# Linear attention, cross attention and a top-1 expert layer: the spreading of the queries over the heads goes from Pool to VectorE

## The chip, the cores and the metric

The kernel runs on one core of one Trainium2 chip. The metric is the device time in microseconds; lower is better. A core has TensorE (PE, matrix products), VectorE (DVE), ScalarE (ACT), GpSimd (POOL), and queues of DMAs, here issued by SyncE (SP) and by Pool. Each engine takes its instructions in the order of its own program, and they meet only in semaphores.

## What is computed

x and the context hold 32 sequences of 128 tokens with 128 features. Three blocks follow each other, each with the residual and a layer norm behind it:

```python
# 1: causal linear attention, 16 heads of 8
q, k = relu(q) + 1e-6, relu(k) + 1e-6
kv    = cumsum(einsum('bhld,bhle->bhlde', k, v), axis=2)
k_cum = cumsum(k, axis=2)
out   = einsum('bhld,bhlde->bhle', q, kv) / maximum(einsum('bhld,bhld->bhl', q, k_cum)[..., None], 1e-6)
x = layernorm(x + out @ out_w.T + out_b)
# 2: cross attention to the context, softmax over keys at most 64 tokens away
x = layernorm(x + softmax(scores(x, ctx)) @ ctx_heads @ W_proj.T + b_proj)
# 3: 8 experts, each token to the best one, at most int(N / E * 1.25) + 1 tokens an expert
top1 = argmax(softmax(xf @ wg)); h = gelu(eb @ W1 + b1); y = h @ W2 + b2
x = layernorm(x + gathered * combine_w)
```

## The kernel before

The kernel is written by hand for each engine, with explicit semaphores. A first stage (up to about 380 us of the span) treats the sequences as a pipeline: round n handles sequence n in its first operations, sequence n - 1 in later ones, down to n - 8. `at(op, n - 2)` in an engine's loop emits the operation for sequence n - 2 if there is one. There are B + LAST = 40 rounds, and the order of the `at` lines is the order in which that engine works. The second stage is the expert layer.

In each round the following matters here (b is the sequence):

- TensorE makes q, k and v of sequence n (`op_qkv`, L567 to L569) into the bank "qkv".
- VectorE turns the bank into qT (L922), kT (L916) and, with the bias, the values V1 (`op_v`, L928).
- Pool spreads qT over the heads: QE (`op_QE`, L420) has 4 copies of qT[128, 128], each multiplied by a column of `head_mask`, so that a product with a group of 32 rows of kT sees one head of 8 rows alone. The two inputs are read with repetition: qT four times, and each of the 4 mask elements 128 times.
- TensorE's scores of the first attention (`op_s1`, L533 with QE and kT) use QE one round later, at n - 1.
- VectorE subtracts the mean and scales for the first layer norm: x1 of sequence n - 2 (`op_x1`, L1002), and for the second, x2 of sequence n - 7 (`op_x2`, L1032). Both are one operation from SBUF to SBUF of 128 x 128 in fp32, with two scalars per partition.
- TensorE transposes x1 (`op_x1T`, L526), then makes pv1 (L589), then the scores of the cross attention s2 (L533 with CE and x1T). VectorE copies the transposed x1 in between (`op_x1Te`, L1088). s2 claims the bank of the transpose too, and so waits for that copy.
- VectorE takes maxima over s2's banks (`op_mx0`, `op_mx1`, L1007) at the start of its next round.
- Pool in each round: x1 + bias (`op_x1b`, L431), the power -1/2 for x1 (L426), xb = X + bias (L409), the copy V2 of the context (L414), QE (L420), the power -1/2 for x2 and for the fallback (L437 to L446), and the scatter of x2 into the experts' rows (L453, a DMA).

VectorE's order around the change is ve1, q, k, lg5, n2, v, x1, x2, rk1, res2, x1Te. Pool's power for x1 waits for ve1 (L977), and xb, V2 and QE follow it. QE has two buffers and `op_q` of the next sequence waits for QE_ready.

Of the kernel before, what the change touches and what calls it, by code (L numbers as in the profile page):

```python
# [8 lines left out]
ALU = mybir.AluOpType  # L9
# [3 lines left out]
P = 128  # L13
# [13 lines left out]
class Seq:  # L27
# [10 lines left out]
    def wait(self, mark=None):  # L38
        self.eng.wait_ge(self.sem, self.n if mark is None else mark)
# [7 lines left out]
def decoder(nc, x, ctx_in, qkv_w, qkv_b, out_w, out_b, proj_w, proj_b, wg, W1, b1, W2, b2, out):  # L47
    B, T, D = x.shape
    E, _, F = W1.shape
    HD = 8  # L50
    H = D // HD
# [3 lines left out]
    NA = H // G  # L55
# [23 lines left out]
    with ctx:  # L79
        def sb(name, shape, dt=F32):  # L80
            return ctx.enter_context(nc.sbuf_tensor(name, shape, dt))

        def ring(name, n, shape, dt=F32):
            return [sb(f"{name}{k}", shape, dt) for k in range(n)]

        def sem(name):
            return ctx.enter_context(nc.semaphore(name))

        banks = ctx.enter_context(nc.psum_tensor("banks", [P, 8, 512], F32))
        BANKS = {name: used for name, _, used in JOBS}  # L90

        def bank(name):
            return banks[:, BANKS[name][0], :]

        def by_parity(V):

            return V[:].rearrange("p (s q) (u w) -> p s (q u) w", q=2, w=SLOT)[:, :, 0:4:3, 0:HD]
# [18 lines left out]
        head_mask = sb("head_mask", [P, NA])  # L116
# [23 lines left out]
        qT = ring("qT", 2, [P, P])  # L140
        kT = ring("kT", 2, [P, P])
        QE = ring("QE", 2, [P, NA, P])
# [102 lines left out]
        qkv_full, q_done, k_done, v_done = sem("qkv_full"), sem("q_done"), sem("k_done"), sem("v_done")  # L245
        QE_ready = sem("QE_ready")
        s1_full = sem("s1_full")
# [45 lines left out]
        def at(op, b):  # L293
            if 0 <= b < B:
                op(b)
# [75 lines left out]
        def _(pool):  # L371
            g = nc.gpsimd
# [41 lines left out]
                g.tensor_copy(by_parity(V2[b % 4]),  # L414
                              C[b % RX][:].rearrange("p (s q d) -> p s q d", q=2, d=HD)).then_inc(v2_ready, 1)

            def op_QE(b):
                pool.wait_ge(q_done, b + 1)
                wait(pool, s1_full, b - 1)
                g.tensor_tensor(QE[b % 2][:], qT[b % 2][:].unsqueeze(1).broadcast_to([P, NA, P]),  # L420
                                head_mask[:].unsqueeze(2).broadcast_to([P, NA, P]), ALU.mult).then_inc(QE_ready, 1)

            def op_pow1(b):
                pool.wait_ge(var1_ready, b + 1)
                wait(pool, x1_ready, b)
                g.tensor_tensor(rs1[:], ve1[:], minus_half[:, 0:1], ALU.pow).then_inc(rstd1_ready, 1)  # L426
# [30 lines left out]
            for n in range(B + LAST):  # L457
                at(op_x1b, n - 4)
                at(op_pow1, n - 2)
                at(op_xb, n)  # L460
                at(op_v2, n - 1)
                at(op_QE, n)
                at(op_pow2, n - 6)
                at(op_fbs, n - 6)
                at(op_scatter, n - 8)
# [416 lines left out]
        def _(dve):  # L882
            v = nc.vector
# [35 lines left out]
            def op_q(b):  # L919
# [2 lines left out]
                v.tensor_scalar(qT[b % 2][:], bank("qkv")[:, 0:P], qk_bias[:, 0:1], FEATURE_EPS, ALU.add,  # L922
                                ALU.max).then_inc(q_done, 1)

            def op_v(b):
                dve.wait_ge(qkv_full, b + 1)
                wait(dve, pv1_full, b - 1)
                v.tensor_tensor(by_parity(V1[b % 2]),  # L928
                                bank("qkv")[:, 2 * P:3 * P].rearrange("p (s q d) -> p s q d", q=2, d=HD),
                                v_bias[:].rearrange("p (s q d) -> p s q d", q=2, d=HD), ALU.add).then_inc(v_done, 1)  # L930
# [174 lines left out]
            for n in range(B + LAST):  # L1105
                at(op_mx0, n - 3)
                at(op_mx1, n - 3)
                at(op_den1, n - 2)
                at(op_rec1, n - 2)
                at(op_mxh, n - 3)  # L1110
                at(op_n1, n - 2)
                at(op_mxs, n - 3)
                at(op_y1Te, n - 2)
                at(op_lg1, n - 8)
                at(op_xTe, n)
                at(op_lg2, n - 8)
                at(op_lg3, n - 8)
                at(op_res1, n - 2)
                at(op_lg4, n - 8)
                at(op_st1, n - 2)  # L1120
                at(op_rec2, n - 4)
                at(op_mv1, n - 2)
                at(op_ve1, n - 2)
                at(op_q, n)
                at(op_k, n)
                at(op_lg5, n - 8)
                at(op_n2, n - 4)
                at(op_v, n)
                at(op_x1, n - 2)
                at(op_x2, n - 7)  # L1130
                at(op_rk1, n - 8)
                at(op_res2, n - 6)
                at(op_x1Te, n - 2)
                at(op_rk2, n - 8)
                at(op_st2, n - 6)
                at(op_rk3, n - 8)
                at(op_mv2, n - 6)
                at(op_rk4, n - 8)
                at(op_ve2, n - 6)
# [115 lines left out]
```

## Time and profile before

| | |
|---|---|
| median of 3 runs | 499.87 us (498.59 to 501.1) |
| the profiled execution: time, span of the core | 499.5 us, 497.6 us |
| busy in the span: TensorE, VectorE, ScalarE, Pool | 425.5, 358.0, 283.5, 247.6 us |
| mean granted clock of TensorE | 0.949 |
| steady rounds 100 to 300 us: TensorE, VectorE, ScalarE, Pool busy | 190.8, 171.4, 133.3, 102.9 of 200 us |
| QE on Pool | 32 times, mean 1032 ns |
| x1 and x2 on VectorE | 32 times each, mean 414 and 883 ns |

A busy engine need not be the bound: the ends of TensorE's products are modelled and overlap. The span leaves out a little at either end of the execution. In a timeline, an operation often starts up to 0.1 us before the one ahead of it on its engine has ended.

### The profile page before, as it was taken

The page shows a single profiled execution, that of the slowest core. Times are in us where ns is not written, and L with a number is a line of the kernel's source. Part 1 is how long each engine was busy: PE and PEld are TensorE (multiplying, and loading weights), DVE is VectorE, ACT ScalarE, POOL GpSimd, SP SyncE. Part 2 cuts the span into 40 slices and gives each one's busy share as a digit, 9 for nine tenths or more (in the row PEclk, how much of TensorE's full clock was granted, in tenths as well). Part 3 has the DMA queues.
Part 4 walks back from the last instruction along what each step waited for, and adds up shares of the span by engine and source line. Part 5 has one row for each costly group of instructions (what it writes and reads, how often), then busy time and mean ns, then how long its engine had stood idle before and what let it go on. Part 6 is the DMA issues. An engine that isn't in the chain of part 4 may idle for free. (4 is left out here: it accounts for less than half of the span.)

```text
span 497.6 us, 20822 instructions
## 1 busy us (share of the span) xinstructions
PE 425.5 (86%) x7767; PEld 335.0 (67%) x7767; DVE 358.0 (72%) x1680; ACT 283.5 (57%) x691; POOL 247.6 (50%) x420
## 2 busy tenths in 40 slices
PE   3879999999999999999999999998851699999930
PEld 2667777777777777777777777775641488888730
DVE  5255677788888788888788888887574267767740
ACT  1445667666766666767666766666242356666620
POOL 4132244554454554454554454553364036887883
PEclk9999999999999999999999999999775699999985
DMA  5700000101000101000101000000004333344100
GB/s 149 237 14 14 24 14 14 29 25 38 27 24 26 29 25 40 25 26 24 30 24 40 26 13 15 19 15 19 13 29 121 84 81 89 101 112 124 24 19 18
DMA packets 30901, 22.69 MB, mean 46 GB/s; under 512 B 4460, under 2 KB 27281, under 8 KB 30804
## 3 DMA queue, kind: packets, MB, share of 16 engines
q1 hardware_dynamic: 27604, 17.16, 12.3%
q0 software_dynamic: 3200, 4.22, 2.9%
q8 instruction: 63, 1.03, 0.9%
q14 instruction: 34, 0.28, 0.2%
HBM read 12.25 MB, written 9.65 MB: 44 GB/s over the span
## 5 line engine op out<-in xcount | busy, mean ns | idle before, releaser
L1007 DVE TENSOR_REDUCE mx<-banks 128x8 f32<-128x1024 f32 x64 | 75.4, 1219 | 37.8 <-PE banks L541 37.8
L797 ACT ACTIVATE arena<-banks 128x1024 f32<-128x1024 f32 x64 | 62.0, 1021 | 35.4 <-PE banks L541 35.4
L426 POOL TENSOR_TENSOR rs<-ve,minus_half 128x1 f32<-128x1 f32 x32 | 18.0, 564 | 115.5 <-DVE ve L977 115.5
L589 PE MATMUL banks<-arena,V 128*32 128x128 f32 x2048 | 70.0, 278 | 0.6 <-ACT arena L797 0.6
L767 ACT ACTIVATE arena<-banks,first_half 128x512 f32<-128x512 f32 x64 | 44.7, 698 | 32.8 <-PE banks L541 32.8
L589 PEld LDWEIGHTS banks<-arena,V 128*32 128x32 f32 x2048 | 52.6, 110 | 11.1 <-issue 8.9
L483 POOL DMA_INDIRECT out_x<-ot,idx x48 | 50.0, 1041 | 12.0 <-issue 10.2
L533 PE MATMUL banks<-CE,x1T 32*128 32x128 f32 x1024 | 37.5, 282 | 10.7 <-DVE x1T L1088 9.7
L437 POOL TENSOR_TENSOR rs<-ve,minus_half 128x1 f32<-128x1 f32 x32 | 17.9, 559 | 56.1 <-DVE ve L996 56.0
L745 PE MATMUL banks<-w_sb,arena 128*112 128x128 f32 (+1 forms) x384 | 44.0, 274 | 0.9 <-issue 0.6
L533 PEld LDWEIGHTS banks<-CE,x1T 32*128 32x128 f32 x1024 | 32.2, 186 | 18.2 <-DVE x1T L1088 16.2
L872 ACT ACTIVATE arena<-banks,b1T 128x321 f32<-128x321 f32 x64 | 33.8, 528 | 18.7 <-PE banks L735 18.0
L745 PEld LDWEIGHTS banks<-w_sb,arena 128*112 128x112 f32 (+1 forms) x384 | 42.1, 173 | 2.9 <-issue 2.4
L533 PE MATMUL banks<-QE,kT 32*128 32x128 f32 x1024 | 38.5, 287 | 2.9 <-DVE kT L916 1.6
L533 PE MATMUL banks<-x1T,CE 32*128 32x128 f32 x1024 | 39.3, 292 | 1.2 <-DVE r L965 0.9
L541 PE MATMUL banks<-later,identb 64*64 64x256 bf16 x512 | 39.8, 285 | 0.0
L533 PEld LDWEIGHTS banks<-QE,kT 32*128 32x128 f32 x1024 | 33.1, 190 | 9.4 <-issue 7.5
L453 POOL DMA_INDIRECT expert_in<-x,sidx x32 | 35.0, 1093 | 8.6 <-issue 5.9
L735 PE MATMUL banks<-arena,w_sb 128*128 128x321 f32 x128 | 38.0, 452 | 0.7 <-DVE arena L1146 0.7
L861 ACT ACTIVATE ot<-r,nm,rs 112x128 f32<-112x128 f32 (+1 forms) x48 | 21.0, 485 | 30.8 <-DVE nm L1208 29.0
L768 ACT ACTIVATE arena<-banks 128x512 f32<-128x512 f32 x64 | 38.5, 602 | 0.0
L785 ACT ACTIVATE CE<-banks,head_mask 128x128 f32<-128x128 f32 x128 | 36.6, 375 | 3.2 <-PE banks L526 3.2
(149 smaller groups left out, 1039.2 us busy)
## 6 DMA issues: line engine op xcount, KB each, us to landing
w_sb<-in_L_ffn_W SPq DMA_DIRECT2D x16, 256.0 KB
expert_in<-zeros SPq DMA_DIRECT2D x10, 273.0 KB, 3.3
EB<-expert_in SPq DMA_DIRECT2D x8, 341.2 KB
X<-in_x SPq DMA_DIRECT2D x32, 64.0 KB, 1.9
C<-in_ctx SPq DMA_DIRECT2D x32, 64.0 KB, 2.3
out_x<-fb SPq DMA_DIRECT2D x32, 64.0 KB
out_x<-ot,idx POOLq DMA_INDIRECT x48
b2b<-in_L_ffn_b SPq DMA_DIRECT2D x1, 512.0 KB, 5.2
```

The costliest lines, as they stand in the source:

```text
L453: g.indirect_dma_start(out=buf, out_offset=bass.IndirectOffsetOnAxis(ap=sidx[b % 4][:], axis=0), in_=x2[b % 4][:], in_offset=None, bounds_ ...
L483: g.indirect_dma_start(out=out.rearrange("b t d -> (b t) d"), out_offset=bass.IndirectOffsetOnAxis(ap=idx[e % 3][0:rows, c:c + 1], axis=0) ...
L533: pe.matmul(banks[:, used, a * P:(a + 1) * P], weights(part, a), moved(part, a), start=first and a == 0, stop=False, tile_position=(VW * j ...
L541: return pe.matmul(view[:, :, cols], identb[at_rows, at_rows], mask, start=False, stop=True, tile_position=(at_rows.start, rows.start))
L589: mm = pe.matmul(bank(name)[VW * s:VW * (s + 1), half * P:(half + 1) * P], V[:, h, :], scored[:, h // NA, h % NA, :], start=q == 0, stop=q ...
L735: pe.matmul(act_bank[j % 4][:, 0:HALF], w1_sb[e % 2][:, f * P:(f + 1) * P], rows[:, half * HALF:(half + 1) * HALF], start=True, stop=True) ...
L745: mm = pe.matmul(max_bank[n % 2][0:rows, 0:D], hT[e % 2][:, f, c * ER:c * ER + rows], w2_sb[e % 2][:, f, :], start=(f == 0), stop=(f == FC ...
L767: nc.scalar.activation(to[:, :, :, 0:W2C], at_bank[:, :, :, 0:W2C], ACT.Relu, scale=first_half[:])
L768: nc.scalar.activation(to[:, :, :, W2C:P], at_bank[:, :, :, W2C:P], ACT.Relu).then_inc(s1_out[half], 1)
L785: last = nc.scalar.activation(CE[b % 4][:, a, :], bank("cT")[:, 0:P], ACT.Copy, scale=head_mask[:, a:a + 1])
L797: nc.scalar.activation(P2[b % 2][:, 2 * half:2 * half + 2].rearrange("p j a t -> p j (a t)"), pair("s2t", half), ACT.Exp, scale=SCALE).the ...
L1007: v.tensor_reduce(mx[b % 2][:, 8 * half:8 * half + 8].rearrange("p (j a) -> p j a", a=NA), pair("s2", half).rearrange("p j (a t) -> p j a ...
```

## The change

QE's operation leaves Pool's program and becomes one of VectorE's, directly behind `op_v` and ahead of `op_x1`. Its inputs, its output and its two waits (on q_done and, for the buffer, on s1_full) stay the same, and so does the semaphore that it raises for TensorE.

```diff
@@ Pool
-            def op_QE(b):
-                pool.wait_ge(q_done, b + 1)
-                wait(pool, s1_full, b - 1)
-                g.tensor_tensor(QE[b % 2][:], qT[b % 2][:].unsqueeze(1).broadcast_to([P, NA, P]),
-                                head_mask[:].unsqueeze(2).broadcast_to([P, NA, P]), ALU.mult).then_inc(QE_ready, 1)
...
                 at(op_v2, n - 1)
-                at(op_QE, n)
                 at(op_pow2, n - 6)
@@ VectorE
+            def op_QE(b):
+                dve.wait_ge(q_done, b + 1)
+                wait(dve, s1_full, b - 1)
+                v.tensor_tensor(QE[b % 2][:], qT[b % 2][:].unsqueeze(1).broadcast_to([P, NA, P]),
+                                head_mask[:].unsqueeze(2).broadcast_to([P, NA, P]), ALU.mult).then_inc(QE_ready, 1)
...
                 at(op_v, n)
+                at(op_QE, n)
                 at(op_x1, n - 2)
```

## Rows read from the trace of the kernel before

**Rows 1.** Waits from 100 to 300 us: total us, times, longest.

```profile
DVE mx L1007 <- PE banks L541: 18.5, 19, 1.1
...
PE banks L533 <- DVE x1T L1088: 7.6, 18, 0.5
```

**Rows 2.** Timeline of VectorE, rounds 13 and 22: start us, us, what.

```profile
137.51 0.36 DVE L1002 TENSOR_SCALAR x<-r,mv,rs 128x128 f32<-128x128 f32 x1
...
233.48 0.41 DVE L1002 TENSOR_SCALAR x<-r,mv,rs 128x128 f32<-128x128 f32 x1
233.81 1.09 DVE L1032 TENSOR_SCALAR x<-r,mv,rs 128x128 f32<-128x128 f32 x1
234.81 0.14 DVE L1035 TENSOR_SCALAR x<-x 128x1 f32<-128x1 f32 x1
...
235.30 0.28 DVE L1088 COPY x1T<-banks 128x128 f32<-128x128 f32 x1
```

**Rows 3.** Timeline of Pool, rounds 13 and 22.

```profile
137.51 0.28 POOL L414 COPY V<-C 128x128 f32<-128x128 f32 x1
...
233.12 0.44 POOL L409 TENSOR_TENSOR xb<-X,outb 128x128 f32<-128x128 f32 x1
233.52 0.28 POOL L414 COPY V<-C 128x128 f32<-128x128 f32 x1
233.77 1.03 POOL L420 TENSOR_TENSOR QE<-qT,head_mask 128x512 f32<-128x512 f32 x1
```

**Rows 4.** Timeline of TensorE, rounds 21 and 22.

```profile
225.27 1.17 PE L533 MATMUL banks<-CE,x1T 32*128 32x128 f32 x32 [0.38 <-DVE x1T L1088]
...
234.13 0.27 PE L526 MATMUL banks<-ident,x 128*128 128x128 f32 x1
...
235.84 1.17 PE L533 MATMUL banks<-CE,x1T 32*128 32x128 f32 x32 [0.42 <-DVE x1T L1088]
...
239.27 1.17 PE L533 MATMUL banks<-QE,kT 32*128 32x128 f32 x32
```

**Rows 5.** Timeline of VectorE and TensorE in round 15.

```profile
159.03 0.98 DVE L1002 TENSOR_SCALAR x<-r,mv,rs 128x128 f32<-128x128 f32 x1
...
160.16 0.30 PE L526 MATMUL banks<-ident,x 128*128 128x128 f32 x1 [0.51 <-DVE x L1002]
...
161.40 1.17 PE L533 MATMUL banks<-CE,x1T 32*128 32x128 f32 x32
```

**Rows 6.** Timeline of Pool, VectorE and TensorE in round 4.

```profile
44.71 0.46 POOL L409 TENSOR_TENSOR xb<-X,outb 128x128 f32<-128x128 f32 x1
44.96 0.34 DVE L1002 TENSOR_SCALAR x<-r,mv,rs 128x128 f32<-128x128 f32 x1
45.10 0.34 POOL L414 COPY V<-C 128x128 f32<-128x128 f32 x1
...
46.83 1.17 PE L533 MATMUL banks<-CE,x1T 32*128 32x128 f32 x32
```

**Rows 7.** Timeline of Pool and VectorE in round 9.

```profile
91.14 0.46 POOL L431 TENSOR_TENSOR x1b<-x,projb 128x128 f32<-128x128 f32 x1
...
91.42 0.23 DVE L1024 TENSOR_TENSOR mxs<-mx,mxs 128x16 bf16<-128x16 f32 x1
```

**Rows 8.** Groups of VectorE: line, operation, output<-input, count | busy us, mean ns | idle before.

```profile
L1007 DVE TENSOR_REDUCE mx<-banks 128x8 f32<-128x1024 f32 x64 | 75.4, 1219 | 37.8 <-PE banks L541 37.8
...
L1166 DVE SCALAR_TENSOR_TENSOR arena<-b2b,EB 112x128 f32<-112x128 f32 (+1 forms) x48 | 13.2, 345 | 0.0
...
L958 DVE TENSOR_TENSOR y<-banks,rden 128x128 f32<-128x128 f32 x32 | 9.1, 284 | 0.0
...
L928 DVE TENSOR_TENSOR V<-banks,v_bias 128x128 f32<-128x128 f32 x32 | 9.0, 282 | 0.0
...
L1024 DVE TENSOR_TENSOR mxs<-mx,mxs 128x16 bf16<-128x16 f32 x32 | 5.2, 163 | 0.0
...
L901 DVE TENSOR_SCALAR minus_head<-lane_pair 128x512 bf16<-128x512 f32 x1 | 0.4, 430 | 0.0
```

## The prediction

> **What bounds the kernel now.** I first looked for the resource that the loop over the sequences waits on, in the list of waits over 100 to 300 us. TensorE has no spare time there but one wait that comes back in nearly every round: the scores of the cross attention (s2, L533) wait for VectorE's copy of the transposed x1 (L1088) [rows 1]. VectorE in turn waits for s2's banks before its maxima (L1007) [rows 1]. So a round is a ring: s2 on TensorE, VectorE's long row of small operations from the maxima down to x1 (L1002), the transpose of x1, the values' product pv1, and s2 again. What moves the start of s2 against the start of x1 moves the whole round. The timelines of one steady round (n = 22) then give the ring's last part: x1 starts at 233.48 and s2 at 235.84, which is 2.36 us [rows 2, 4]. Two s2 starts lie 10.57 us apart [rows 4].
>
> What the reader should see in these rows is one operation that is too long. x2 (L1032) takes 1.09 us, and x1, the same operation on the same shape, 0.41 us here and 0.34 us in an early round [rows 2, 6]. x2 ends at 234.90, 0.10 us behind the end of Pool's QE (233.77 + 1.03 = 234.80) [rows 3]. x1's 0.41 us ends at 233.89, 0.09 us behind the end of Pool's V2 copy (233.80) [rows 3]. In round 15 x1 came late enough to meet QE itself and took 0.98 us [rows 5]. So while Pool runs an operation from SBUF to SBUF, these VectorE operations stand still. An operation between two SBUF tensors did so once too: mxs (L1024) took 0.23 us beside Pool's x1b and ended 0.05 us behind it, where its mean is 0.16 us [rows 7, 8].
>
> The Trainium skill (SBUF — State Buffer, the section on two separate sides) says the same: the pair of ports is an exclusive lock for a whole instruction, and it names VectorE operations with two SBUF inputs too, against a Pool operation that reads SBUF. The trace agrees, with the 1.09 us for one input; for two inputs it has the one mxs row. By this rule QE is held up by xb and, if it comes second, by V2; without it the sum below would be the 501.8 us of rival 2.
>
> **What the change removes.** Pool loses 32 operations of 1.03 us [rows 3]. Pool waits for VectorE in every round, so its own time is worth nothing. QE's reader, s1 of the next round on TensorE (239.27), starts over 4 us after QE is ready [rows 4]; the new QE is ready no later than the old (about 234.2 against 234.8), so s1 gains or loses nothing. No DMA is issued by QE, and the queues are untouched. What counts is that x2 is free: its step from start to start falls from 1.00 us (233.81 to 234.81) [rows 2] to about 0.26 us, as 0.34 us less the 0.08 us by which a VectorE operation starts ahead of its forerunner's end (233.89 - 233.81).
>
> **What it adds.** One operation of 512 columns on VectorE ahead of x1, with x1, x2, the ranks, r2 and the copy of x1T queued behind it. No such operation is in the trace. The maxima take 1219 ns for 1024 columns and the values' bias 282 ns for 128 [rows 8]: 1.046 ns a column, so 0.68 us for 512, and 0.60 us from start to start. The bounds are 0.43 us (minus_head, 512 columns, one input) [rows 8], and 1.03 us, Pool's own time for it [rows 3]. I take 0.68: the maxima and the bias run on the engine that QE goes to, and minus_head reads one tensor where QE reads two. The mask is read with one element repeated 128 times; n2 (L958) repeats each factor 8 times and costs 284 ns against 282 [rows 8], so I charge nothing for that.
>
> The Trainium skill (VectorE: DVE Perf Modes, the section on the TRN2 errata) gives 691 ns for an fp32 tensor_tensor of 512 columns. By it the sum below would be 0.2 to 0.3 us longer.
>
> **A steady round (24 of them, n = 8 to 31).** QE starts where x1 started, 233.48. x1 starts 0.60 later, at 234.08, and needs 0.34: 234.42. From the end of x1 to its transpose on a waiting TensorE is 0.15 us, and from there to s2, where the copy isn't late, 1.24 us (160.01 to 160.16 to 161.40) [rows 5]. So s2 starts at 235.81 against 235.84: 0.03 us earlier. Is the copy late? x2 starts at 234.34, the next at 234.60, and the copy 0.49 later (234.81 to 235.30 now) at 235.09, ends at 235.37, and s2 could follow 0.26 later (235.58 to 235.84 now), at 235.63. It isn't. The wait of 0.4 us ahead of s2 is thus not won: it moves in front of the transpose of x1, as TensorE now reaches it at 234.13 [rows 4] and gets it at 234.57. What is late next is pv1. 24 x -0.03 = -0.7 us.
>
> **Who gets SBUF first.** QE meets Pool's xb, which ends at 233.56, and V2, which starts at 233.52 [rows 3]. A VectorE operation seems to ask for SBUF some time after its start. x1 ends 0.09 us after it is let in, so it asks 0.34 - 0.09 = 0.25 behind its start. QE would end 0.54 (512 columns) + 0.03 after it is let in, the 0.03 from mxs (0.05 less 0.02 for 16 columns) [rows 7]; so it asks 0.68 - 0.57 = 0.11 to 0.12 behind its start. In round 4 x1 asked at 45.21 and won against V2, which started at 45.10 and took 0.34 instead of 0.28 [rows 3, 6]; so V2 asks about 0.11 behind its start. QE asks at 233.60, xb is out at 233.56 and V2 asks at about 233.63: QE wins by 0.03 us. If V2 wins, QE ends at 233.80 + 0.57 = 234.37 instead of 234.16: 0.2 us lost. In three of the 15 rounds that I read, V2 starts together with x1 instead of 0.04 behind it (as at 137.51) [rows 2, 3], and there it may win: I charge 3 x 0.20 = +0.6 us.
>
> **The early rounds (n = 2 to 7, six).** Here there is no x2 in Pool's way (x2 of sequence 0 comes in round 7), so nothing is given back. Round 4: QE would start at 44.96; xb ends at 45.17, so QE ends at 45.17 + 0.57 = 45.74. x1 runs from 45.66 to 46.00, and s2 starts 1.39 later (as 160.01 to 161.40) at 47.39 instead of 46.83 [rows 5, 6]: +0.55 us. The others are alike: 6 x 0.55 = +3.3 us. Rounds 0 and 1 have no x1 and lose nothing; the expert stage is not touched.
>
> **Sum.** 3.3 - 0.7 + 0.6 = +3.2 us. The profiled execution took 499.5 us (span 497.6), so 502.7 us; from the median of the runs, 499.87 us, it would be 503.1. I take the middle, 499.7 + 3.2 = 502.9 us: slower by 0.6%. About 0.5%, 2.5 us, is what a measurement of this kernel can tell from no change (its three runs span 498.59 to 501.1).
>
> **Rivals.**
> 1. V2 wins the race in every steady round. For it: the margin is 0.03 us. Against: x1 in round 4. Then 24 x 0.17 = +4.1 and 3.3: +7.4 us, 507.1 us. Chance 0.22.
> 2. A VectorE operation with two SBUF inputs does not wait for Pool. For it: only one mxs row shows it waiting, and the 48 gate products of the expert stage (L1166) never stretch, mean 345 ns [rows 8]. Then QE ends 0.1 us earlier in an early round, which loses 0.46, and there is no race: 2.8 - 0.7 = +2.1 us, 501.8 us. Chance 0.12.
> 3. On the other side, QE runs as fast as minus_head: 0.43 us, 0.35 from start to start. That is 0.25 less in 30 rounds, -7.5 us: 3.2 - 7.5 = -4.3, 495.4 us. TensorE could take it, as it reaches the transpose 0.44 us earlier than it is served. It decides for faster when the step is under 0.60 - (3.2 + 2.5)/30 = 0.41 us. Against it: minus_head has one tensor input, QE two. Chance 0.08. The Trainium skill (VectorE: DVE Perf Modes, the perf-mode tier table) allows tensor_tensor in fp32 only one element a cycle, which speaks against this rival.
> 4. The repeated element slows the reading and QE takes up to Pool's 1.03 us: 30 x 0.35 = +10.5 on top, 513.4 us. Chance 0.06.
>
> **How the numbers follow.** My forecast has 0.48, with its own range 501 to 505 us: 30 rounds by 0.06 us up or down, what the rows' rounding and the race leave open; 0.04 is left for what I don't see. The bound of 502.4 us cuts the forecast: about 0.34 of it is slower, 0.14 the same. Slower by over 0.5%: 0.34 + 0.22 + 0.06 = 0.62, less a little for unseen gains, 0.60. Same: 0.14 + 0.12 and half of the unseen, 0.30. Faster: 0.10. The range leaves out rivals 3 and 4 and takes in rivals 1 and 2: 500.0 to 508.5 us.
>
> **What the profile after would show.** QE on VectorE at 0.68 us, x2 at 0.34 us in all rounds, and Pool's V2 stretched by about 0.5 us or more in the steady rounds (if V2 keeps 0.28 and QE takes 0.88, rival 1 is right; if neither stretches, rival 2). The wait of s2 for the copy of x1T is gone, and one of about 0.4 us for x1 (L1002) stands in front of the transpose. Steady rounds stay at 10.5 to 10.6 us, and rounds 2 to 7 are each about half a microsecond longer. I am wrong if QE's step isn't 0.60 us, or if the early rounds have slack that I took for none.

## The result, and the profile after

The changed kernel takes 511.25 us (median of four runs, 510.15 to 512.8) against 500.31 us (498.59 to 501.1): a ratio of 1.0236 [1.0205, 1.0268], slower by 10.9 us where 3.2 were forecast, and outside the forecast's range of 500.0 to 508.5 us. The profiled execution took 510.15 us with a span of 508.2. Busy time of each engine on its page:

```profile
span 508.2 us, 20822 instructions
PE 429.8 (85%) x7767; PEld 337.0 (66%) x7767; DVE 358.1 (70%) x1712; ACT 286.9 (56%) x691; POOL 229.6 (45%) x388
```

VectorE's busy time is the same as before (358.0 us): it took QE over and lost the standstill of x2. The groups of the first 380 us show this (line, operation, output<-input, count | busy us, mean ns | idle before):

```profile
L414 POOL COPY V<-C 128x128 f32<-128x128 f32 x32 | 23.5, 736 | 0.0
L921 DVE TENSOR_TENSOR QE<-qT,head_mask 128x512 f32<-128x512 f32 x32 | 22.7, 710 | 0.0
...
L802 ACT COPY yx<-banks 128x256 f32<-128x256 f32 x32 | 11.9, 372 | 34.6 <-PE banks L582 34.6
L1001 DVE TENSOR_SCALAR x<-r,mv,rs 128x128 f32<-128x128 f32 x32 | 10.9, 342 | 0.7 <-POOL rs L420 0.7
L1031 DVE TENSOR_SCALAR x<-r,mv,rs 128x128 f32<-128x128 f32 x30 | 10.6, 353 | 0.0
```

QE has a mean of 0.71 us, x2 0.35 (before 0.88), and Pool's V2 copy now takes 0.74 instead of 0.28 [rows 3]: it is V2 that stands still. Line numbers are 1 to 7 lower than before (L533 is L526, L589 is L582, L1002 is L1001). A steady round (n = 22), from the timelines of all engines (start us, us, what, [wait]):

```profile
241.24 0.68 DVE L921 TENSOR_TENSOR QE<-qT,head_mask 128x512 f32<-128x512 f32 x1
241.29 0.79 POOL L414 COPY V<-C 128x128 f32<-128x128 f32 x1
...
241.84 0.34 DVE L1001 TENSOR_SCALAR x<-r,mv,rs 128x128 f32<-128x128 f32 x1
242.10 0.34 DVE L1031 TENSOR_SCALAR x<-r,mv,rs 128x128 f32<-128x128 f32 x1
242.33 0.30 PE L519 MATMUL banks<-ident,x 128*128 128x128 f32 x1 [0.28 <-DVE x L1001]
...
243.57 1.17 PE L526 MATMUL banks<-CE,x1T 32*128 32x128 f32 x32
...
245.38 1.08 PE L582 MATMUL banks<-arena,V 128*32 128x128 f32 x32
...
246.26 1.10 POOL L447 DMA_INDIRECT expert_in<-x,sidx  x1 [0.21 <-issue]
...
246.89 0.37 ACT L802 COPY yx<-banks 128x256 f32<-128x256 f32 x1 [1.07 <-PE banks L582]
...
247.36 1.17 PE L526 MATMUL banks<-QE,kT 32*128 32x128 f32 x32 [0.39 <-ACT yx L802]
```

Up to s2 (243.57) every row is where the prediction put it: QE 0.68 us, x1 0.60 behind it, s2 2.33 behind QE's start instead of 2.36 [rows 2, 4]. The loss lies behind s2. There TensorE makes pv2 (L582), the same product as pv1 for the second attention, and ScalarE copies its result (yx2, L802); s1 needs that copy. From s2 to the next s1 it is 247.36 - 243.57 = 3.79 us, where before it was 239.27 - 235.84 = 3.43 [rows 4]. s1 waits for yx2, and yx2 waits for pv2 (started at 245.38): it starts 1.51 us behind pv2's start, which in an undisturbed round is 1.15. Pool's scatter starts 0.88 us behind pv2's start, while pv2 runs. The waits from 100 to 300 us (total, times, longest) say the same:

```profile
ACT yx L802 <- PE banks L582: 18.4, 18, 1.1
...
PE banks L526 <- ACT yx L802: 6.1, 16, 0.4
PE banks L519 <- DVE x L1001: 5.4, 19, 0.5
...
PEld banks L526 <- DVE x1T L1087: 0.3, 1, 0.3
```

The wait of s2 for the copy of x1T is gone [rows 1], and one for x1 is there instead, as foreseen; 6.1 us of a wait of s1 for yx2 are new (before 0.4, once). In 22 of the 24 steady rounds yx2 comes at 1.48 to 1.56 us behind pv2's start and the round takes about 10.87 us; in the two others the scatter starts at 1.06 and 1.08, yx2 comes at 1.15 and the round takes 10.53. One of the two:

```profile
180.67 1.08 PE L582 MATMUL banks<-arena,V 128*32 128x128 f32 x32
181.75 1.09 POOL L447 DMA_INDIRECT expert_in<-x,sidx  x1 [0.21 <-issue]
181.82 0.37 ACT L802 COPY yx<-banks 128x256 f32<-128x256 f32 x1 [0.72 <-PE banks L582]
```

The kernel before had its scatter at 1.06 in nearly every round. Its round 15, of which [rows 5] show the first part, is the exception among the steady rounds, and is disturbed in the same way; these are its rows behind s2:

```profile
163.21 1.08 PE L589 MATMUL banks<-arena,V 128*32 128x128 f32 x32
...
164.08 1.10 POOL L453 DMA_INDIRECT expert_in<-x,sidx  x1 [0.21 <-issue]
164.71 0.37 ACT L809 COPY yx<-banks 128x256 f32<-128x256 f32 x1 [1.07 <-PE banks L589]
...
165.18 0.57 PE L533 MATMUL banks<-QE,kT 32*128 32x128 f32 x9 [0.39 <-ACT yx L809]
```

The first two rounds behind the steady ones, in which the pipeline empties, show it too in this kernel: with the scatter at 0.79 yx2 comes 2.16 us behind pv2's start, with 0.93 at 1.53. The first of them:

```profile
343.10 1.08 PE L589 MATMUL banks<-arena,V 128*32 128x128 f32 x32
343.89 1.09 POOL L453 DMA_INDIRECT expert_in<-x,sidx  x1 [0.21 <-issue]
345.26 0.37 ACT L809 COPY yx<-banks 128x256 f32<-128x256 f32 x1 [1.73 <-PE banks L589]
```

Why is the scatter earlier? VectorE's work for x2's variance (ve2, L995) follows x2, which is now short. ve2 stands 0.28 us behind s2's start instead of 0.45, and Pool's power, the fallback's three operations and the scatter follow from ve2. So the gain of x2 arrives on Pool 0.17 to 0.19 us earlier and puts the scatter onto pv2.

### The profile page after: what moved, and what is told of

The parts are those of the page before. It is cut to its first block, busy times and chain, and to the rows that moved or that the text cites. A ratio compares the mean times of both kernels' runs of the same rounds, so it can differ in the third digit from the quotient of the medians.

```text
span 508.2 us, 20822 instructions
## 1 busy us (share of the span) xinstructions
PE 429.8 (85%) x7767; PEld 337.0 (66%) x7767; DVE 358.1 (70%) x1712; ACT 286.9 (56%) x691; POOL 229.6 (45%) x388
## 3 DMA queue, kind: packets, MB, share of 16 engines
q8 instruction: 63, 1.03, 0.9%
## 4 chain that ended last, share of the span: by engine, by line
PE 47%; DVE 20%; issue 18%; POOL 7%; ACT 2%; DMA 2%; DVEq 1%; SPq 1%; POOLq 0%; ACTq 0%
PE banks L526 16%; PE banks L582 14%; PE banks L519 7%; POOL out_x L476 6%; PE banks L534 5%; DVE QE L921 3%; POOL rs L466 2%; DVE r L964 2%; ACT yx L802 2%; DVE x L1001 2%; PE banks L728 1%; DVE rden L952 1%; DVE mx L1006 1%; DVE V L927 1%; DVE cand L1048 1%
## 5 line engine op out<-in xcount | busy, mean ns | idle before, releaser
L582 PE MATMUL banks<-arena,V 128*32 128x128 f32 x2048 | 70.4, 279 | 0.6 <-ACT arena L790 0.6
L582 PEld LDWEIGHTS banks<-arena,V 128*32 128x32 f32 x2048 | 52.7, 111 | 10.0 <-issue 5.1
L476 POOL DMA_INDIRECT out_x<-ot,idx x48 | 50.0, 1042 | 12.0 <-issue 10.5
L526 PE MATMUL banks<-QE,kT 32*128 32x128 f32 x1024 | 38.7, 287 | 10.1 <-ACT yx L802 8.4
L526 PEld LDWEIGHTS banks<-QE,kT 32*128 32x128 f32 x1024 | 33.3, 190 | 16.6 <-issue 14.8
L526 PE MATMUL banks<-x1T,CE 32*128 32x128 f32 x1024 | 39.2, 291 | 1.2 <-ACT mxT L753 0.8
L526 PE MATMUL banks<-CE,x1T 32*128 32x128 f32 x1024 | 38.5, 287 | 0.9 <-ACT arena L790 0.8
L526 PEld LDWEIGHTS banks<-CE,x1T 32*128 32x128 f32 x1024 | 32.3, 190 | 7.5 <-issue 6.1
```

Of the source, the lines that this page charges most:

```text
L476: g.indirect_dma_start(out=out.rearrange("b t d -> (b t) d"), out_offset=bass.IndirectOffsetOnAxis(ap=idx[e % 3][0:rows, c:c + 1], axis=0) ...
L526: pe.matmul(banks[:, used, a * P:(a + 1) * P], weights(part, a), moved(part, a), start=first and a == 0, stop=False, tile_position=(VW * j ...
L582: mm = pe.matmul(bank(name)[VW * s:VW * (s + 1), half * P:(half + 1) * P], V[:, h, :], scored[:, h // NA, h % NA, :], start=q == 0, stop=q ...
```

## Experiments

Below, "scatter at 0.87" means a start 0.87 us behind pv2's start, and the "late end" that pv2's result reaches ScalarE later than 1.15 us behind pv2's start. Where nothing else is said, such values are those of the 24 steady rounds. The kernels ran in four batches, each on a chip of its own, beside the kernel before: 499.06, 502.1, 501.09 and 499.77 us. No chip was used in two batches, so where this text says "chip", it could also be something else that differed from batch to batch. The chip of the first measurement is not on record. That the chip matters was not suspected until the third batch, and the expectations of the first two are written without it.

### First batch: where the scatter starts, and where QE stands

e1: the changed kernel with Pool's addition x1b ahead of the scatter instead of first in the next round; all else alike.

```diff
-                at(op_x1b, n - 4)
                 at(op_pow1, n - 2)
...
                 at(op_fbs, n - 6)
+                at(op_x1b, n - 3)
                 at(op_scatter, n - 8)
```

> Theory (scatter): in the changed kernel Pool's scatter starts 0.87 us behind the start of pv2, which is before pv2 is done (1.08), where it started at 1.06 in the kernel before; the signals of TensorE that fall into its first 0.6 us arrive late, so the copy yx2 starts 1.49 instead of 1.15 us behind pv2 and s1 0.34 us later. With x1b put ahead of the scatter on Pool, the scatter starts at about 1.35, yx2 is back at 1.15, steady rounds take 10.53 instead of 10.87 us, and the kernel about 503.5 us. Rival (TensorE): the signal is late because TensorE no longer pauses between pv1 and s2 and runs behind its own queue; then the place of the scatter doesn't matter, rounds stay at 10.87 and the time at 511 us.

Measured: 502.51 us, 1.0077 [1.0051, 1.0104]. Scatter at 1.25 or 1.26 (twice at 1.44 and 1.46), yx2 at 1.15 in every round, steady rounds 10.53 us.

e2: the kernel before, with the scatter earlier by one small Pool operation. It leaves out the addition of the layer norm's 1e-5 to the variance of the fallback rows (the expectations of e8, e12 and e15, which leave out the same operation, write 1e-6).

```diff
-                own.mark(g.tensor_scalar(fbe[:], fbv[:], LN_EPS, None, ALU.add))
-                own.wait()
...
-                g.tensor_tensor(fbs[b % 4][:], fbe[:], minus_half[:, 0:1], ALU.pow).then_inc(fbs_ready, 1)
+                g.tensor_tensor(fbs[b % 4][:], fbv[:], minus_half[:, 0:1], ALU.pow).then_inc(fbs_ready, 1)
```

> The kernel before, in which Pool's addition of the layer norm's 1e-5 for the fallback rows (fbe) is left out, so that the scatter starts about 0.35 us earlier, at 0.7 us behind pv2's start. Scatter theory: yx2 starts 0.2 to 0.35 us later in each of 24 rounds, 505 to 508 us. Rival (TensorE): the pause in front of s2 is still there, nothing changes, 500.3 us.

Measured: 499.46 us, 0.9995 [0.9973, 1.0016]. Scatter at 0.73, as intended, but yx2 at 1.15 in every round. The scatter theory missed this, and I took to a second condition (the place of TensorE's pause ahead of s2). That was wrong, as the third batch shows.

e3 and e4: QE on VectorE, but directly behind x1 (e3), or behind the copy of the transposed x1 (e4).

```diff
-                at(op_QE, n)
                 at(op_x1, n - 2)
+                at(op_QE, n)          # e3
                 at(op_x2, n - 7)
...
                 at(op_x1Te, n - 2)
+                at(op_QE, n)          # e4
```

> QE on VectorE, behind x1 instead of ahead of it. Both theories: x1 isn't delayed, the early rounds lose nothing; x2 costs 0.26 and QE 0.60 us where the blocked x2 cost 1.00, so the copy of x1T and with it s2 come 0.2 us earlier in 24 rounds. ve2 and the scatter move with s2, so the scatter stays at 1.06 and no signal is late: about 495.5 us, rounds of 10.36 us.

> QE on VectorE, behind the copy of x1T. The copy comes about 0.8 us earlier than in the kernel before, so s2 follows pv1 at once, 0.47 us earlier in 24 rounds. Scatter theory: ve2 moves by only 0.2 us, so against pv2 the scatter comes later (about 1.3 us) and no signal is late: 10.1 us a round, about 489 us. Rival (TensorE): without the pause in front of s2 the signal of pv2 is 0.34 us late and most of the gain is lost: 10.4 us a round, about 497 us.

Measured: e3 495.45 us, 0.9925 [0.9901, 0.9949], steady rounds 10.41 us. e4 486.75 us, 0.9741 [0.9709, 0.9772], steady rounds 10.06 us. No yx2 was late in either, though e3 had scatters at 0.97 and 0.92 in two rounds.

### Second batch: the control, and the scatter moved again

e5: the changed kernel, unaltered.

> The changed kernel once more, unaltered, as the control beside the other three. Theory 1 (the late end of pv2 belongs to the order of this kernel: the pause lies ahead of the transpose of x1, and Pool's scatter starts 0.87 to 1.01 us behind pv2's start): the yx2 copy is again 1.48 to 1.51 us behind pv2's start in nearly all steady rounds, 10.87 us a round, 510 to 512 us. Rival (the late end belonged to the one execution environment of the first measurement and not to the order): yx2 at 1.15, rounds of 10.53 us, 502 to 503 us; then the experiments with a moved scatter told nothing.

Measured: 510.73 us, 1.0178 [1.0128, 1.0229], yx2 at 1.47 to 1.55, scatter at 0.86 to 0.90 (once 0.99) in 22 of 24 steady rounds. The first measurement is confirmed.

e7: the changed kernel with a small operation ahead of the scatter.

```diff
             def op_scatter(b):
+                own.wait()
+                own.mark(g.memset(nudge[:], 0.0))
```

> The changed kernel with one small Pool operation (a memset of 128x1) ahead of the scatter, which should start it 0.1 to 0.4 us later, 1.0 to 1.3 us behind pv2's start; nothing else moves, the bias addition for x1 included, which stays behind the scatter. Theory 1: from a start of 1.02 us on there is no late pv2, steady rounds of 10.53 us, 502.5 to 503.5 us. Rival 1 (it is not the scatter but the order of x1b and scatter, which the experiment with the later scatter also changed): the late pv2 stays, 510.5 to 512 us.

Measured: 511.8 us, 1.0216 [1.0155, 1.0278]. It tells nothing new: the memset (0.10 us) ran in the idle time of Pool that there is ahead of each scatter, and the scatter still started at 0.87 to 0.89; yx2 was as late (once, with a scatter at 0.82, at 2.20).

e8: the changed kernel with e2's edit (the addition of 1e-5 left out).

> The changed kernel without the addition of the 1e-6 to the variance of the fallback rows (that part of the computation is left out), so that the scatter starts 0.33 us earlier, at about 0.54 us behind pv2's start, with the pause still ahead of the transpose of x1. Theory 1 as a threshold (any scatter that starts before pv2 is done holds its end back): the late pv2 stays, 510.5 to 512 us. Theory 1 as a window (only a start 0.8 to 1.01 us behind pv2's does it): yx2 at 1.15 and 10.53 us a round, 502.5 to 503.5 us, as the one round of the before kernel's variant with a scatter at 0.54 was undisturbed.

Measured: 524.48 us, 1.0424 [1.0357, 1.0491]; scatter at 0.54 to 0.76, yx2 at 1.96 to 2.13, most rounds 11.34 to 11.40 us. The window of the expectation falls, and so does the threshold's figure of 510.5 to 512 us: with the scatter at 0.54 pv2's end is later than with 0.87. But the end doesn't move steadily with the scatter: in the two steady rounds with 0.74 and 0.76 yx2 comes at 2.12 and 2.13.

```profile
199.37 1.08 PE L580 MATMUL banks<-arena,V 128*32 128x128 f32 x32
199.91 1.08 POOL L445 DMA_INDIRECT expert_in<-x,sidx  x1 [0.23 <-issue]
...
201.37 0.37 ACT L800 COPY yx<-banks 128x256 f32<-128x256 f32 x1 [1.56 <-PE banks L580]
```

e9: e4 with the last power of the fallback (L440) moved behind the scatter (`op_fbs` split in two).

```diff
+                at(op_fbv, n - 6)
                 at(op_scatter, n - 8)
+                at(op_fbs, n - 6)
```

> The kernel with QE behind the copy of the transposed x1 (486.75 us, scatter 1.40 us behind pv2's start, no pause between pv1 and s2) with the last power of the fallback moved behind the scatter, so that the scatter starts about 0.50 us earlier, at about 0.90 us. Theory 1 (no pause between pv1 and s2, and the scatter in the window): yx2 goes to 1.48 to 1.51 and some 24 rounds become 0.31 to 0.34 us longer: 494 to 495 us. Rival 1 (the late pv2 needs QE ahead of x1 on VectorE, by something that the trace does not show): 486 to 488 us.

Measured: 491.31 us, 0.9788 [0.9735, 0.9841]. The scatter came to 1.05 to 1.07, not to 0.90, and yx2 stayed at 1.15; in the one steady round with a scatter at 1.00 it was at 1.58. In six more rounds, with the scatter at 1.05 or 1.06 as in most of the others, yx2 was on time, but the transposes that follow pv2 on TensorE (L597) came late: VectorE's den (L940), the divisor of the first attention, starts 2.40 us behind pv2's start instead of 2.03. These six rounds took 10.34 to 10.63 us, while most of the others took 10.06. One such round, and behind it one in which den isn't late:

```profile
193.05 1.09 POOL L449 DMA_INDIRECT expert_in<-x,sidx  x1 [0.54 <-issue]
...
194.39 0.17 DVE L940 TENSOR_SCALAR den<-banks 128x16 f32<-128x16 f32 x1 [0.28 <-PE banks L597]
...
203.41 1.10 POOL L449 DMA_INDIRECT expert_in<-x,sidx  x1 [0.54 <-issue]
...
204.38 0.17 DVE L940 TENSOR_SCALAR den<-banks 128x16 f32<-128x16 f32 x1
```

So the kernel with QE behind the copy is open to the late end as well; its scatter at 1.40 is what keeps it clear.

### Third batch: the same kernels on one chip

e8 and e2 have the same edit, in the changed kernel and in the kernel before, and one was disturbed and the other wasn't. They had run on different chips.

> The changed kernel, unaltered, for the third time, beside three kernels whose first runs had no late pv2 on another chip. The first batch of variants and the second ran on different chips, and the before kernel's variant with a scatter at 0.73 us behind pv2's start was undisturbed in the first while the changed kernel's variant with 0.54 us lost 0.85 us a round in the second. Theory A (the late end of pv2 exists on some chips only, and there for every kernel whose scatter starts before pv2 is done): on a chip with it 510 to 512 us and yx2 at 1.49; on a chip without it 502 to 503.5 us, yx2 at 1.15 and steady rounds of 10.53 us. Theory B (it belongs to the order alone, on every chip): 510 to 512 us wherever it runs.

> The changed kernel with the bias addition for x1 moved ahead of the scatter (scatter 1.26 us behind pv2's start) once more, now beside the changed kernel itself. Theory A: 502 to 503.5 us and yx2 at 1.15 on either kind of chip, as the scatter starts behind pv2's end. Rival (its 502.51 us of the first time was only the chip): 510 us or more, with the late yx2, where the changed kernel beside it has it too.

> The kernel before without the addition of the 1e-6 to the fallback's variance (that part is left out), scatter 0.73 us behind pv2's start, once more. Theory A on a chip where the changed kernel shows the late pv2: yx2 at scatter + 1.4 = 2.1 us, about 0.95 us more in 24 rounds, 520 to 525 us; on a chip where the changed kernel beside it shows none: 499 to 500 us as before. Theory B (the order ahead of s2 decides): 499 to 500 us on either kind, since its pause lies between pv1 and s2.

> QE behind the copy of the transposed x1 once more (scatter 1.40 us behind pv2's start). Theory A: 486 to 488 us and no late yx2 on either kind of chip. Rival: 10 us more where the changed kernel shows the late pv2.

| | kernel | us | ratio | scatter, yx2 behind pv2 |
|---|---|---|---|---|
| e10 | changed | 511.39 | 1.0249 [1.0175, 1.0323] | 0.87 to 0.89, 1.47 to 1.50 (once 1.00, 1.56; at 1.06 and 1.08, 1.15) |
| e11 | as e1 | 503.19 | 1.0039 [1.0019, 1.006] | 1.26, 1.15 |
| e12 | as e2 | 521.58 | 1.0399 [1.0361, 1.0436] | 0.73 to 0.76, 2.09 to 2.13 (once 0.88, 1.49; once 0.55, 2.00) |
| e13 | as e4 | 488.54 | 0.9736 [0.9693, 0.9778] | 1.41, 1.15 |

All four came out as theory A has it, the late end on some chips only, and there for every kernel whose scatter starts before pv2 is done (e13 is 0.5 us above its range). In the emptying rounds e13 shows the late end too: with the scatter at 0.79 yx2 is at 2.15, where e4, the same kernel on the first batch's chip, has 0.79 and 1.15. The kernel that took 499.46 us in the first batch takes 521.58 here, with the same instructions at the same distances up to the scatter. A round of e12:

```profile
193.43 1.08 PE L587 MATMUL banks<-arena,V 128*32 128x128 f32 x32
194.17 1.08 POOL L451 DMA_INDIRECT expert_in<-x,sidx  x1 [0.23 <-issue]
...
195.52 0.37 ACT L807 COPY yx<-banks 128x256 f32<-128x256 f32 x1 [1.66 <-PE banks L587]
...
195.99 1.17 PE L531 MATMUL banks<-QE,kT 32*128 32x128 f32 x32 [0.98 <-ACT yx L807]
```

It isn't the data of the scatter: between 194.17 and 195.80 the DMA view of this run has

```profile
DMA packets 0, 0.00 MB, mean 0 GB/s; under 512 B 0, under 2 KB 0, under 8 KB 0
```

and the scatter's 32 packets come behind that. Nor is it Pool's being busy: in e11, on this chip, the addition x1b runs in the very place of the scatter (0.63 to 1.09 us behind pv2's start) and nothing is late. Nor is it the order of x1b and the scatter, which e11 also changed: e12 leaves that order alone.

### Fourth batch: the changed kernel on a chip without the late end

> The changed kernel, unaltered, on whichever chip comes. Theory A (late end of pv2 on some chips only): if this is a chip of the first batch's kind, yx2 is 1.15 us behind pv2's start in every round although the scatter starts at 0.87, steady rounds are 10.53 us and the time is 502 to 503.5 us; if it is one of the kind of the other three, 510 to 512 us and 1.49. Theory B (the order decides, on every chip): 510 to 512 us and 1.49 on any chip, also where the variant beside it with a scatter at 0.73 us is undisturbed.

> The kernel before without the addition of 1e-6 to the fallback's variance (left out), scatter at 0.73 us, as the probe of the chip beside the changed kernel: 521 us and yx2 at 2.1 on a chip with the late end, 499.5 us and 1.15 on one without. Theory A: it and the changed kernel are either both disturbed or both undisturbed.

Measured: e15, the probe, 500.08 us, 1.0004 [0.9967, 1.004], scatter at 0.74 and yx2 at 1.15, so this chip is of the first batch's kind. A round of it:

```profile
238.05 1.08 PE L587 MATMUL banks<-arena,V 128*32 128x128 f32 x32
238.79 1.08 POOL L451 DMA_INDIRECT expert_in<-x,sidx  x1 [0.23 <-issue]
...
239.20 0.37 ACT L807 COPY yx<-banks 128x256 f32<-128x256 f32 x1 [0.72 <-PE banks L587]
```

e14, the changed kernel, took 502.75 us (501.81 to 505.87) beside 499.77: 1.0056 [1.0011, 1.0101], 3.0 us slower. Its scatter starts at 0.87, and yx2 at 1.15 (once 1.16) in every round:

```profile
241.43 1.08 PE L582 MATMUL banks<-arena,V 128*32 128x128 f32 x32
...
242.30 1.09 POOL L447 DMA_INDIRECT expert_in<-x,sidx  x1 [0.21 <-issue]
...
242.57 0.37 ACT L802 COPY yx<-banks 128x256 f32<-128x256 f32 x1 [0.72 <-PE banks L582]
...
243.04 1.17 PE L526 MATMUL banks<-QE,kT 32*128 32x128 f32 x32
```

## Why the prediction was right in its steps and wrong in its time

- **QE's cost: right.** 0.68 us where nothing holds it, 0.60 from start to start. Rivals 3 (0.43 us) and 4 (1.03 us) fell. The Trainium skill (VectorE: DVE Perf Modes, the section on the TRN2 errata) gives 691 ns for it; the rows agree, with 0.68 us.
- **The early rounds: right.** QE is held by Pool's xb, and s2 starts come 10.35 to 10.39 us apart (49.97 to 60.36 below) instead of 9.83 to 9.86 (as 46.83 [rows 6] to 56.65): +0.51 us a round where 0.55 was forecast. QE took 0.75 us here, not 0.78. So a VectorE operation with two SBUF inputs does wait for Pool, and rival 2 fell. Of the six rounds charged, four such gaps show the price; the gap ahead of them (28.12 to 39.62) varies from 9.8 to 14.8 us between the runs, and what it waits for stays open.

```profile
47.33 0.45 POOL L409 TENSOR_TENSOR xb<-X,outb 128x128 f32<-128x128 f32 x1
47.58 0.75 DVE L921 TENSOR_TENSOR QE<-qT,head_mask 128x512 f32<-128x512 f32 x1
47.72 0.76 POOL L414 COPY V<-C 128x128 f32<-128x128 f32 x1
...
60.36 1.17 PE L526 MATMUL banks<-CE,x1T 32*128 32x128 f32 x32
```

- **The race with V2: right, and a little better.** QE starts 0.04 or 0.05 us ahead of V2 (once 0.01) and wins in 23 of the 24 steady rounds; once (284.80), with V2 0.01 us ahead, it took 0.82 us and V2 kept 0.28. Three such rounds were charged (+0.6 us), one came. Rival 1 fell.
- **The steady round up to s2: right.** x1 to s2 as worked out, no wait for the copy, 0.03 us less. On the chip without the late end a steady round takes 10.53 us instead of 10.56, and the whole kernel 3.0 us more than before, where the sum was 3.2. The interval of that 3.0 runs from 0.5 to 5.0 us, so how close the two figures lie is in part luck.
- **The step that failed: "Steady rounds stay at 10.5 to 10.6 us".** They take 10.87 us in the first measurement and on the chips of the second and third batch. The prediction followed x2's gain only as far as s2's path and gave it a worth of nothing elsewhere ("Pool waits for VectorE in every round, so its own time is worth nothing"). It didn't ask what a shorter x2 lets Pool start earlier: the scatter, 1.06 to 0.87 us behind pv2's start. On these chips pv2's end, as ScalarE sees it, then comes 0.34 us late. 22 rounds of 0.34 are 7.5 us, nearly all of the 511.25 - 502.75 = 8.5 us that lie between the two kinds of chip.
- **The missed warning.** Round 15 of the kernel before ([rows 5]) was read for the step from x1 to s2 alone. Further down, s1 waits 0.39 us for yx2, the one wait of its kind in 200 us. The rows at 343.10 in the section on the result show yx2 as much as 1.0 us late. With these rows the price of an early scatter (0.35 us a round at 0.87) was to be had from the trace; not that other chips don't charge it.
- **Why e4 is faster than both.** QE behind the copy of x1T frees x1, x2 and Pool, and needs 0.68 us in a place where VectorE would wait for s2's banks anyway. x1 to s2 falls from 2.36 to 1.86 us (226.75 to 228.61, in e13). 24 rounds of 0.50 are 12 us, and 501.09 - 488.54 is 12.6.

```profile
226.75 0.41 DVE L1001 TENSOR_SCALAR x<-r,mv,rs 128x128 f32<-128x128 f32 x1
226.79 0.28 POOL L414 COPY V<-C 128x128 f32<-128x128 f32 x1
...
227.08 0.34 DVE L1031 TENSOR_SCALAR x<-r,mv,rs 128x128 f32<-128x128 f32 x1
...
228.02 0.68 DVE L921 TENSOR_TENSOR QE<-qT,head_mask 128x512 f32<-128x512 f32 x1
...
228.61 1.17 PE L526 MATMUL banks<-CE,x1T 32*128 32x128 f32 x32
```

**What stays open.** By what the scatter holds pv2's end back, and in what the chips differ. The trace shows the starts of TensorE's products unmoved and their consumers late. Not pv2's alone: in the round of 245.38 VectorE's den waits 0.17 us for the transposes behind pv2, and the load of X, which waits for the transpose of C, is issued 0.61 us behind that transpose's start, 0.47 in e14. The semaphore events that the trace keeps beside the instructions put the delay on TensorE's side: in that round its signal for pv2 comes 1.48 us behind pv2's start (1.12 in e14), the one for the transpose of C at 1.52 (1.38) and the one for the transposes behind it at 2.25 (1.59), while VectorE's signal for its first maxima comes at 0.99 in both. Whether TensorE itself stood still or only its signals were held back isn't shown. And since each chip was measured in one batch alone, no run tells the chip from the batch.

## What to carry to other kernels

When an operation gets shorter, follow it to every engine that waits for it, also to those with time to spare, and look at what they then start beside the critical work; here a gain of 0.19 us on an idle Pool cost 0.34 us a round on TensorE, in the first measurement and on two of four chips. A single odd round in the trace of before is a free experiment: read it to its end. And before two variants that ran on different chips are compared, run one of them, or the changed kernel itself, on both.

## What the runs showed of the hardware

- On the chips of the second and third batch, and in the first measurement, work on TensorE that is under way when Pool starts an indirect DMA ends late for those who wait for it. In the steady rounds, with a start 0.86 to 1.01 us behind pv2's start, yx2 starts 0.55 to 0.65 us behind the scatter's start; at 0.82 and below (e7 once, e8, e12), 1.35 to 1.47 us behind it. From 1.05 us on yx2 is at 1.15, but in e9 the transposes behind pv2 were still late in six of 24 rounds (den at 2.40 instead of 2.03); in e11, with 1.25 and more, nothing is late. On the chips of the first and fourth batch, starts from 0.54 to 1.00 have no effect (e2, e3, e14, e15). The Trainium skill (SBUF — State Buffer, the section "Who interferes with whom") says that "PE and ACT never wait on anyone". It speaks of the ports of SBUF; the chips of e1 and e14 agree, with yx2 at 1.15 us, and whether the late end of the others, up to 2.1 us, is such a wait no run here shows.
- A QE on VectorE and a V2 on Pool that overlap cost the later one most of the other's time: V2 0.79 instead of 0.28 us, 0.51 us beside a QE of 0.68. The same section of the Trainium skill calls the shared ports an exclusive lock for the whole instruction, and this trace agrees.
- Of two such operations, the one that started 0.04 us or more ahead won in all rounds (22 of 24 steady ones here). At about 0.01 us ahead by the trace it won in both cases here and lost in one of e1 (at 279.00).
